# Codes of a quantised attention written as 16-bit integers and read as fp16, the scaling of the row maxima on VectorE, and a program without a barrier behind its first loads

## The reference

```python
def _fq(x, delta, zp, n_bits):
    xi = _round_ste(x / delta) + zp
    xq = jnp.clip(xi, 0.0, 2.0 ** n_bits - 1.0)
    return (xq - zp) * delta
...
sim = jnp.einsum('bhid,bhjd->bhij', _fq(q, dq, 128.0, 8), _fq(k, dk, 128.0, 8)) * SCALE
attn = jax.nn.softmax(sim, axis=-1)
out = jnp.einsum('bhij,bhjd->bhid', _fq(attn, dw, 0.0, 8), _fq(v, dv, 128.0, 8))
```

## Time and profile before

| | |
|---|---|
| median of 3 runs | 1584.53 us (1580.52 to 1589.36) |
| the profiled execution's own time | 1576.92 us |
| its span, 28607 instructions | 1575.1 us |
| PE, PE weight loads | 1092.8 us (69%), 593.3 us (38%) |
| DVE, ACT, POOL busy | 1098.1 us (70%), 894.2 us (57%), 681.1 us (43%) |
| mean DMA traffic | 74 GB/s |

### The profile page before, as it was taken

One profiled execution on the slowest core, in us unless ns is written; L12 is line 12 of the kernel. 1 busy time (PEld: TensorE's weight loads), 2 busy tenths in 40 slices (PEclk: granted clock), 3 DMA queues, 4 the chain that ended last, 5 costly groups with the idle time before them and its releaser, 6 DMA issues.

```text
span 1575.1 us, 28607 instructions
## 1 busy us (share of the span) xinstructions
PE 1092.8 (69%) x9344; PEld 593.3 (38%) x9344; DVE 1098.1 (70%) x3102; ACT 894.2 (57%) x2546; POOL 681.1 (43%) x1055
## 2 busy tenths in 40 slices
PE   2888888887788797855353545444358778888888
PEld 1333344444333286831120212222225435453545
DVE  2687777777688653678888999877765666666522
ACT  1555554555554464567676797988852344646531
POOL 3321011011011416558888888877741344445310
PEclk9899999999999998975555555555569799999989
DMA  5213142101331112267555576665530121201000
GB/s 184 61 53 92 51 129 75 54 24 50 99 106 49 42 39 82 57 160 122 99 104 109 106 130 115 121 109 106 109 57 14 27 48 35 49 21 43 1 0 27
DMA packets 265219, 116.53 MB, mean 74 GB/s; under 512 B 216936, under 2 KB 253936, under 8 KB 262896
## 3 DMA queue, kind: packets, MB, share of 16 engines
q1 hardware_dynamic: 260112, 108.29, 30.8%
q0 software_dynamic: 2048, 4.20, 0.9%
q10 hardware_dynamic: 2912, 2.22, 0.5%
HBM read 38.80 MB, written 16.45 MB: 35 GB/s over the span
## 4 chain that ended last, share of the span: by engine, by line
PE 35%; POOL 21%; DVE 18%; issue 14%; ACT 9%; DMA 1%; SPq 0%; POOLq 0%; another core or an unknown queue 0%; ACTq 0%; DVEq 0%
POOL arena L2289 12%; ACT arena L1581 4%; PE acc L1199 3%; POOL inv_total L2278 2%; PE trans L1171 2%; DVE minus_top L1980 2%; PE misc L1021 2%; PE misc L1027 2%; PE trans L1323 2%; ACT arena L1528 2%; PE score L1335 2%; PE score L1337 2%; PE trans L1177 1%; POOL arena L2235 1%; PE acc L1385 1%
## 5 line engine op out<-in xcount | busy, mean ns | idle before, releaser
L2289 POOL TENSOR_SCALAR arena<-arena,inv_total 128x512 f16<-128x512 f32 (+1 forms) x512 | 299.7, 585 | 57.3 <-DVE inv_total L2058 16.8
L1980 DVE TENSOR_REDUCE minus_top<-score 128x4 f32<-128x616 f32 (+4 forms) x256 | 200.6, 802 | 95.3 <-PE score L1141 36.9
L2154 POOL TENSOR_TENSOR rstd<-spread,minus_half 128x4 f32<-128x4 f32 x36 | 37.5, 1043 | 489.5 <-DVE spread L1662 414.0
L1581 ACT ACTIVATE arena<-score,minus_top,exp_scale 128x512 f32<-128x512 f32 (+1 forms) x340 | 210.4, 625 | 20.9 <-POOL arena L2289 11.9
L1528 ACT ACTIVATE arena<-trans 128x512 f32<-128x512 f32 x240 | 134.4, 596 | 109.3 <-PE trans L1177 104.0
L1619 ACT ACTIVATE arena<-arena,minus_top 128x154 f32<-128x154 f32 x256 | 105.2, 412 | 129.3 <-DVE minus_top L2123 129.1
L1280 PE MATMUL score<-arena 32*128 32x512 bf16 (+1 forms) x340 | 68.9, 458 | 139.7 <-ACT arena L1581 138.7
L2064 DVE TENSOR_REDUCE top_score<-score 128x2 f32<-128x1024 f32 (+1 forms) x128 | 135.7, 1061 | 0.6 <-PE score L1280 0.5
L2309 POOL TENSOR_TENSOR arena<-arena,inv_total 128x512 f32<-128x512 f32 x64 | 66.5, 1040 | 143.9 <-DVE inv_total L2131 130.0
L1581 ACT ACTIVATE arena<-trans,minus_top,exp_scale 128x154 f32<-128x154 f32 (+1 forms) x172 | 105.5, 620 | 19.2 <-POOL arena L2289 14.9
L2118 DVE CUSTOM_DVE_ANT_0 arena<-score,arena 128x154 f32<-128x154 f32 x256 | 65.9, 313 | 60.6 <-PE score L1360 60.2
(11 more groups left out here) (283 smaller groups left out, 2814.4 us busy)
## 6 DMA issues: line engine op xcount, KB each, us to landing
arena<-q_terms SPq DMA_DIRECT2D x88, 128.0 KB, 2.8
late<-arena SPq DMA_DIRECT2D x128, 64.0 KB, 2.0
q_terms<-arena SPq DMA_DIRECT2D x36, 128.0 KB
late<-k_terms SPq DMA_DIRECT2D x32, 128.0 KB, 3.1
arena<-arena SPq DMA_TRANSPOSE x192, 3.1
by_expert<-zeros SPq DMA_DIRECT2D x2, 1472.0 KB, 9.8
arena<-by_expert SPq DMA_DIRECT2D x10, 256.0 KB
from_expert<-arena SPq DMA_DIRECT2D x10, 256.0 KB
```

What stands on the lines that cost most here:

```text
L1581: ins = nc.scalar.activation(probs[:, i % 3, j, of], quant_score[i % 3][:, j, of], ACT.Exp, bias=minus_top[:, at_col:at_col + 1], scale=ex ...
L1980: nc.vector.tensor_reduce(dst, src, axis=AX.X, op=ALU.max, negate=True).then_inc(top_ready, 1)
L2289: ins = nc.gpsimd.tensor_scalar(codes[:, (i - 1) % CODE_SOURCES, j, to], probs[:, (i - 1) % 3, j, of], inv_total[:, at_col:at_col + 1], HA ...
```

## The change

1. **Codes.** POOL's L2289 computes `probs` times the reciprocal, cut at 255 (multiply, minimum in place of multiply, add), and writes it into the same buffer seen as unsigned 16-bit integers. The DMA transposes the bits as before. PE reads them as fp16 numbers, where a small integer n is n times 2 to the minus 24 (`CODE_STEP`); `out_scale` takes that factor back, and v's codes are fp16. `copy_codes` and its place in DVE's stream go, and PE waits for the transpositions themselves.
2. **Maxima.** ACT's L1572 goes. DVE does it behind its reduction, as a multiplication by `exp_scale` that waits for the reduction.
3. **The start.** One block in place of two, with semaphores for what needs what: PE's first transposes wait for ident, ctx and x, K for the first weights. ACT makes a one-element copy early and issues the loads of the other sequences behind it. The 8 late loads stand on SP behind the first stacked reads. ACT issues half of the `q_first` reads. POOL adds the biases to x of sequences 0 and 1 (item "base") later than before.

```diff
-HALF_ROUND = 1024.0
+CODE_STEP = 2.0 ** -24
...
-                at(exact, f + 1, ("x", nxt), ("pads", nxt))
+                at(exact, f + 1, ("x", nxt), ("pads", nxt), ("base", 0), ("base", 1))
...
-        v_quant, v_quant_tail = put([P, 2, TILES, HEADS, 32], bf16), put([P, 2, HEADS, 32], bf16)
+        v_quant, v_quant_tail = put([P, 2, TILES, HEADS, 32], fp16), put([P, 2, HEADS, 32], fp16)
...
+        code_numbers = codes.rearrange("p i j k -> p (i j k)").bitcast(mybir.dt.uint16)
...
-                        read_queries(slice(0, 2), q_first)
+                        read_queries(slice(0, 2), q_first, slice(0, PRODUCTS // 2))
                     read_queries(slice(0 if u else 2, PAIRS), q_stacked)
                     if u == 0:
+                        for dst, src in late_loads:
+                            sp.dma_start(dst, src).then_inc(late_in, 16)
...
-                    pe.wait_ge(codes_copied, 2 * n + 2)
+                    for i in (2 * n, 2 * n + 1):
+                        pe.wait_ge(codes_turned[i % CODE_SLOTS], 16 * (i // CODE_SLOTS + 1))
...
+                act.wait_ge(first_use_set, 1)
+                nc.scalar.copy(first_use[:, 1:2], first_use[:, 0:1])
...
+                act.wait_ge(q_out, 48)
+                for n in range(PRODUCTS // 2, PRODUCTS):
+                    act.dma_start(q_stack[n::PRODUCTS, 0, 0:2, :], scratch["q"].ap()[:, Q_TERMS[n], 0:2, :]).then_inc(q_first, 16)
...
                     act.wait_ge(quant_top, i + 1)
-                    nc.scalar.activation(of_step(minus_top, i), of_step(top_score, i), ACT.Copy,
-                                         scale=exp_scale[:, of:of + 1]).then_inc(quant_top_scaled, 1)
...
-                        nc.vector.tensor_reduce(of_step(top_score, i), src, axis=AX.X, op=ALU.max,
-                                                negate=True).then_inc(quant_top, 1)
-                    if QUANT_LAG <= i < quant_steps + QUANT_LAG:
-                        copy_codes(i - QUANT_LAG)
+                        then(nc.vector.tensor_reduce(of_step(top_score, i), src, axis=AX.X, op=ALU.max, negate=True))
+                        of = stage(QUANT_STEPS[i][0]) - QSELF
+                        nc.vector.tensor_scalar(of_step(minus_top, i), of_step(top_score, i), exp_scale[:, of:of + 1], None,
+                                                ALU.mult).then_inc(quant_top, 1)
...
-                              inv_total[:, at_col:at_col + 1], HALF_ROUND, ALU.mult, ALU.add)
+                              inv_total[:, at_col:at_col + 1], 255.0, ALU.mult, ALU.min)
```

191 lines of the change are left out of this document (96 added, 95 removed).

## The result

The changed kernel takes **1911.03 us** (median of 4 runs, 1903.36 to 1911.35) beside 1582.53 us before (4 runs on the same chip, 1577.49 to 1589.36): ratio 1.2061, 95% interval 1.2004 to 1.2117, so 329 us slower. The prediction said 1556 us, 1532 to 1576. Its forecast was wrong, and the case that came true is the rival with the slow form of POOL's codes, which had 12%.

A forecast was written before the change was run, and what follows sets the result against it. It took waits on POOL alone to bound QSELF, ACT's exponentials (33.0%) and POOL's codes (15.0%) to lead QCROSS. Gains 8 + 5 + 5 + 5 + 6.7 = 29.7, taken as 28, gave 1556 us, range 1532 to 1576.

The forecast's parts named there:

- the rival with the slow form of POOL's codes: L2289 in both quantised stages: minimum or integer write off POOL's fast path, 128x512 at 1.59 us, kernel 1857 us; 12%.
- POOL's codes, L2289: POOL's code operation in both quantised stages: new second operation and output type change nothing from 692 ns at 128x512.
- Both bounds: For L2289's new duration: no change from its own old row, or L2188's 675 ns for 154 columns.
- The rule that was cited: POOL's integer write: every converted element passes float32 and one converter, so the new output type costs nothing.
- `copy_codes` goes: DVE's copy in the quantised stages: its removal relieves POOL, gaining 8 us in QSELF and 5 in QCROSS.
- The maxima: Scaling moved from ACT to DVE, 0.3 us in QSELF, 0.25 in QCROSS: gains 5 us in each stage.
- the scaling becomes the wait: DVE's scaling waits for POOL's piece and holds the next reciprocal: only 10 us gained in all, 1574.5 us; 19%.
- The start: Kernel start: 5.2 us from earlier first matmul, 2.5 from shared read issue, 1 lost to bulk loads; gain 6.7 us.
- fp16 weights at PE: PE's products in the quantised stages: reading fp16 in place of bf16 costs 0, 5 us in all at worst.
- The sum of all but the minimum: Whole kernel: gains of 29.7 us, taken as 28 because two gains sometimes cover the same idle time.
- What the profile should show: Signs: codes 690 to 705 ns in QSELF, below 430 in QCROSS; scaling 0.2 to 0.35 us; QCROSS unit 37.5.

The follow-up runs named there:

- f16_min: The changed kernel with POOL's codes still multiply, minimum 255.0, but written as fp16 numbers instead of unsigned 16-bit integers: 1908.42 us in one run.
- u16_add: The changed kernel with an addition of 0.0 in place of the minimum in POOL's codes, integers kept: 1541.43 us, ratio 0.9796 to the kernel before.
- mult_alone: The changed kernel with POOL's codes as one multiply by the scalar from SBUF, no second operation: 1761.22 us in one run.
- f16_step: The changed kernel with POOL's codes as multiply, multiply by 2 to the minus 24, written as fp16: 1540.69 us, ratio 0.9790 to the kernel before.
- codes_only: The kernel before with codes as small fp16 numbers (multiply, multiply by 2^-24) and no copy on DVE; start and maxima as before: 1548.15 us, ratio 0.9835.
- start_bulk_first: The kernel before with the start's part of the change alone, but bulk loads issued right behind the small ones: 1572.76 us, ratio 0.9991.

## Why the prediction was wrong

**The step that failed** is in "POOL's codes, L2289": "I take no change, since input, scalar and output width are those of the near row; the far one is a rival." The output type did cost nothing (698 ns with integers). The minimum cost 256 x (2001 - 698) + 256 x (812 - 400) ns = 334 + 105 = 439 us of POOL's time. Of that, some 367 us reach the end (f16_min less u16_add, on the same chip: 1908.42 - 1541.43). By the stages: QSELF goes from (979.5 - 681.3) / 127 = 2.35 us a step in u16_add to 4.67, 295 us in all; from its last L2285 to the last code of QCROSS it is 1503.3 - 1288.3 = 215 us against 1124.2 - 979.5 = 144.7, 70 us. The starts of u16_add:

```profile
L2297 POOL TENSOR_SCALAR arena<-arena,inv_total x512: 393/553/931, 681.7 to 1124.2; 128x512 uint16<-128x512 f32 x86, 128x154 uint16<-128x154 f32 x85
...
L2285 POOL TENSOR_SCALAR inv_total<-inv_total,inv_sizes x128: 283/292/548, 681.3 to 979.5; 128x2 f32<-128x2 f32 x128
```

The argument behind the step was wrong as well. Likeness of operands made L2289's old row the "nearest", but what decides is the pair of operations. Both bounds had been read rightly; L2188 was not a row for odd operands but one for the form without an add, and `mult_alone` shows that L2289 itself falls on its line.

**The rival** had the place and the mechanism right: the codes off their fast path, POOL on the chain in both stages. Its price was too low. It took the rate of a lone operation, 2.55 ns a column, for a pair: 1.59 us and 0.67 us against 2.00 and 0.81 measured; 1857 us against 1911. A lone operation in that place does give nearly its number (1571 and 679 ns), but 1761 us, since the 222 + 57 us were counted as if none of it lay beside other work, and of the gains elsewhere the sum had the start's alone. Its chance of 12% was too small for a form no row showed, on the line that leads the chain: the sentence "the only tensor_scalar of POOL here with 16-bit input and no second operation shows that a slow form exists" named the right evidence. What was set against it, that L2289 keeps "its two operations", was no protection: it matters which two they are.

**The rule that was cited**, one converter for every type (the Trainium skill, "GPSIMD: programming the Q7 cores", Data Types and Layout), agrees with the runs: uint16 and fp16 take 698 and 697 ns. It was silent on the operation, and that silence was not priced.

**The other terms**, read from u16_add, f16_step and the parts:
- *`copy_codes` goes.* Forecast 8 + 5 us, measured 26 (20 to 32) in codes_only. By the stages 22.6 and 4.8 us. QCROSS is as forecast. In QSELF the term was mis-sized: it counted 60% of what POOL gets back, and 22.6 arrives, more than all that POOL is busy less (15.5); the rest is POOL waiting less, and DVE's own relief of 0.58 us a step had been priced only as far as it makes room for the scaling. The reading "its 29 ns on a mean of 692 is far less than a whole instruction" took a mean for the mechanism: in the trace of before, 78 of the 90 copies of QSELF that begin inside a code operation end 277 to 282 ns behind its end, and eight code operations that begin 84 to 87 ns ahead of a copy last 969 to 973 ns and not 692. Each time one waits for the other's work to end, mostly DVE: its copies last 595 ns in QSELF on average, and some 410 where they don't wait.
- *The maxima.* Forecast a gain of 5 + 5 us. With the copy gone QSELF loses 11.3 and QCROSS gains 12.1. In QSELF the step that failed is "with ACT 0.3 and DVE 0.18 shorter I give back 5": DVE's scaling takes 491 ns and not 300, and with the maxima it ends 61.8% of the waits late in QSELF. That is the rival "the scaling becomes the wait", hidden under the slow codes of this kernel. In QCROSS "I take 5, with POOL at 0.40 a piece up to 9" was too low.
- *The start.* Forecast 6.7, measured 3.9 (0 to 8). In the trace the first scores are 7.9 us earlier, near the 5.2 + 2.5 = 7.7 worked out, but that is luck: with the bulk loads kept in front the same two steps bring 33.09 - 28.42 = 4.7 us (start_bulk_first), and the other 2.9 come from the place of the bulk loads, which the sum had as a loss of 1.
- *fp16 weights at PE*: 0 forecast. The products L1299 of before take 307 ns each, and L1253 in u16_add 307:

```profile
L1253 PE MATMUL acc<-arena 128*32 128x128 f16 x1536 | 58.9, 307 | 22.5 <-DVE oT L2057 13.2 <-DMA arena<-arena 9.3
```

- *The sum of all but the minimum*: 28 forecast, 32 measured (26 to 38), out of one term at double and one at nothing. Its size came out near by errors that cancel.

**What the profile should show.** The prediction's own tripwire, "a code operation above 750 ns makes the forecast wrong at once", was crossed at 2001 ns. In u16_add the others stand: codes at 698 and 400 ns (690 to 705 and below 430 forecast), the QSELF step 2.35 us (2.3 to 2.35), a QCROSS unit 144.7 / 4 = 36 us (37.5), while the scaling, at 0.49 us against 0.2 to 0.35 forecast, came up to its own tripwire of 0.5 and did cost its term in QSELF.

## What to carry to other kernels

Before you change the operation of an instruction that leads the chain, ask which row shows that operation, not which row shows those operands; where none does, one timing of the instruction by itself is worth more than any argument, and without it the slow case needs a chance in proportion to what leads the chain. On POOL keep tensor_scalar (one tensor, one or two operations with a scalar each) to pairs of multiply and add on hot lines, add a 0 or multiply by 1 where a lone operation stands, and put a clamp elsewhere. And decide a move of small work between engines stage by stage: here the same 0.3 us cost 11 us in the stage where DVE was the busier engine and gave 12 where ACT was; the sum hid both.
